# A four-layer graph network on one core: the gate computed first, edge terms gathered in layer 0, counts rounded by two instructions, waited values masked

## What is computed

```python
h = jnp.maximum(_layernorm(x), 0.0)
x = x + _L0_gnn_ref(h, src, dst, ...)       # relu((h + segment_sum(h[src], dst)) @ W1 + b1) @ W2 + b2
h = jnp.maximum(_layernorm(x), 0.0)
x = x + _L1_gnn_ref(h, edge_attr_64, ...)   # attention over the edges, 8 heads, softmax per target
h = jnp.maximum(_layernorm(x), 0.0)
x = x + _L2_gnn_ref(h, ...)                 # h @ w_self.T + mean of neighbours @ w_neigh.T
h = jnp.maximum(_layernorm(x), 0.0)
x = x + _L3_gnn_ref(h, src, dst, edge_weight, ...)   # segment_sum(edge_weight * h[src], dst) @ W + b
```

## Time and profile before

| | |
|---|---|
| three runs, without the profiler | 5042.48, 5067.97, 5065.54 us; median 5065.54 |
| the profiled execution | span 5145.3 us from its first to its last instruction; the page gives no other time of it, and it is 79.8 us above the median |
| PE, PEld, DVE, ACT, POOL busy | 75%, 53%, 74%, 30%, 53% of the span |
| mean granted clock of TensorE | 0.909 |
| DMA | 912 MB, 177 GB/s |

### The profile page before, as it was taken

One profiled execution on the slowest core, in us unless ns is written; L12 is line 12 of the kernel. 1 busy time (PEld: TensorE's weight loads), 2 busy tenths in 40 slices (PEclk: granted clock), 3 DMA queues, 4 the chain that ended last, 5 costly groups with the idle time before them and its releaser, 6 DMA issues. The chain is left out here.

```text
span 5145.3 us, 93266 instructions
## 1 busy us (share of the span) xinstructions
PE 3841.6 (75%) x26234; PEld 2720.9 (53%) x26235; DVE 3822.7 (74%) x6359; ACT 1550.3 (30%) x3023; POOL 2737.6 (53%) x2300
## 2 busy tenths in 40 slices
PE   4685555550199968888888888888886348889999
PEld 2443222220189835555555555555554248888888
DVE  3516999991299989999999999999996699970000
ACT  2372234560101130122333444445552430020000
POOL 3430199996732227777777777777776232210000
PEclk8799999995599989999999999999997569999999
DMA  9674423346155444454555666666665535568887
GB/s 168 175 234 111 97 100 126 159 175 198 66 193 209 163 140 106 120 146 142 157 165 169 184 184 188 193 196 197 205 204 159 186 113 200 200 213 300 298 297 254
DMA packets 594376, 912.02 MB, mean 177 GB/s; under 512 B 107452, under 2 KB 519442, under 8 KB 575022
## 3 DMA queue, kind: packets, MB, share of 16 engines
q1 hardware_dynamic: 413024, 521.23, 31.2%
q10 hardware_dynamic: 117359, 250.68, 13.4%
q0 software_dynamic: 63872, 138.75, 11.3%
HBM read 608.33 MB, written 311.94 MB: 179 GB/s over the span
## 5 line engine op out<-in xcount | busy, mean ns | idle before, releaser
L1964 POOL DMA_INDIRECT at_qg<-q_d,at_slot x1616 | 1601.2, 991 | 495.8 <-issue 492.2
L986 PE MATMUL bw_ps<-bw_mov,bw_sta 128*128 128x392 bf16 x7056 | 1590.0, 349 | 19.2 <-issue 7.2
L986 PEld LDWEIGHTS bw_ps<-bw_mov,bw_sta 128*128 128x128 bf16 x7056 | 640.4, 102 | 365.0 <-issue 95.6
L2007 PE MATMUL at_psk<-at_kp,at_hot 128*128 x4848 | 611.7, 234 | 286.8 <-DVE at_qg L2085 244.4
L1051 POOL DMA_INDIRECT tv_rows<-ed_d,tv_place x101 | 628.2, 6219 | 339.1 <-DMA edv_d<-tv_rows 211.0
L2007 PEld LDWEIGHTS at_psk<-at_kp,at_hot 128*128 128x128 bf16 x4848 | 439.1, 101 | 624.1 <-issue 418.1
L889 PE MATMUL ba_ps<-ba_mov,ba_sta 128*128 128x392 bf16 x1968 | 380.4, 338 | 352.6 <-DVE ba_sta L830 309.1
L874 DVE TENSOR_SCALAR ba_mov<-iota,key,scale 128x392 bf16<-128x392 f16 x1968 | 592.4, 365 | 2.8 <-PEq L853 2.8
L970 DVE TENSOR_TENSOR bw_sta<-bw_raw,kw 128x1024 bf16<-128x1024 bf16 x882 | 561.2, 689 | 0.0
L830 DVE TENSOR_TENSOR bw_mov<-bw_ps,lo 128x3136 bf16<-128x3136 f16 x294 | 523.4, 1780 | 7.6 <-PE bw_ps L986 5.4
L1566 PE MATMUL at_p3t<-tile,room 128*128 128x256 f32 (+1 forms) x2450 | 524.2, 376 | 4.6 <-ACT room L1150 4.6
(11 more groups left out here) (537 smaller groups left out, 4668.3 us busy)
## 6 DMA issues: line engine op xcount, KB each, us to landing
tile<-adw_d SPq DMA_DIRECT2D x23, 6272.0 KB, 18.7
adw_d<-xall ACTq DMA_DIRECT2D x65, 1568.0 KB
adj_d<-ba_stage ACTq DMA_DIRECT2D x50, 1568.0 KB, 5.1
l0raw<-adj_d SPq DMA_DIRECT2D x50, 1568.0 KB, 6.6
tile<-adj_d SPq DMA_DIRECT2D x50, 1568.0 KB, 6.5
adw_d<-bw_stage ACTq DMA_DIRECT2D x33, 1568.0 KB
at_rel<-rel_d SPq DMA_DIRECT2D x101, 512.0 KB
et_attr<-in_edge_attr SPq DMA_DIRECT2D x48, 1024.0 KB
```

Of the source, the lines that this page charges most:

```text
L986: ins = pe.matmul(self.ps[:, bass.DynSlice(place, WCOL)], self.sta[:, k, u // 2, :, u % 2], self.mov[:, u // 2, :, u % 2], start=False, st ...
L1964: pool.indirect_dma_start(out=qg[:, ring, b, :], out_offset=None, in_=q_d[:, :], in_offset=bass.IndirectOffsetOnAxis(ap=slot[:, ring, b:b ...
L2007: ins = pe.matmul(ps_k[:, at:at + KW], hot[:, par, sum(ROUNDS[:r]) + u, :], kp[:].rearrange("p j k n -> p (j k n)")[:, bass.DynSlice(place ...
```

## The change

Five things are changed.

- **The gate first.** `load_gate` is called ahead of `mask_rows`, with a semaphore of its own; POOL starts the counts' stage with the gate; SP waits for the store of the gate.
- **The gathers in layer 0.** `terms_by_visits` becomes a class with two buffers in place of four. POOL issues two gathers in each step of layer 0 behind its own three instructions (and its loop over the steps is written out), ACT stores them to `edv_d` at the head of its next step, in place of SP.
- **Rounding by two instructions**, in both layers with counts: one over 48 blocks, one over the last.
- **Masks.** The register values that PE and ACT wait for are masked with 2^14 - 1 first, in the counts and in the weights.
- The first weights' semaphore no longer covers the gate's inputs.

```diff
-        pe.wait_ge(self.s_clear, reg)
+        pe.wait_ge(self.s_clear, reg & TABLE)
...
-                act.wait_ge(self.s_vis, ends[k % half] + self.ring)
+                act.wait_ge(self.s_vis, (ends[k % half] & TABLE) + self.ring)
...
+class TermsByVisits:
+
+
+    def places(self):
+        wait(self.nc.gpsimd, self.c.V(self.nc.vector.tensor_copy(self.place[:], self.c.index[:, :, UK])))
+
+    def gather(self, g):
+        pool, k, lap = self.nc.gpsimd, g % self.ring, g // self.ring
         if lap:
-            pool.wait_ge(s_kept[k], 16 * lap)
-        pool.indirect_dma_start(out=rows[:, k, :], out_offset=None, in_=c.ed_d[:, :], in_offset=bass.IndirectOffsetOnAxis(ap=place[:, g:g + 1], axis=0)).then_inc(s_got[k], 16)
-        sp.wait_ge(s_got[k], 16 * lap + 16)
-        sp.dma_start(c.edv_d[g], rows[:, k, :]).then_inc(s_kept[k], 16)
-    for k in range(ring):
-        sp.wait_ge(s_kept[k], 16 * len(range(k, NG2, ring)))
+            pool.wait_ge(self.s_kept[k], 16 * lap)
+        pool.indirect_dma_start(out=self.rows[:, k, :], out_offset=None, in_=self.c.ed_d[:, :], in_offset=bass.IndirectOffsetOnAxis(ap=self.place[:, g:g + 1], axis=0)).then_inc(self.s_got[k], 16)
+
+    def keep(self, g, k, lap):
+        act = self.nc.scalar
+        act.wait_ge(self.s_got[k], 16 * lap + 16)
+        act.dma_start(self.c.edv_d[bass.DynSlice(g, 1), :, :].rearrange("a p n -> (a p) n"), self.rows[:, k, :]).then_inc(self.s_kept[k], 16)
+
+    def kept(self):
+        for k in range(self.ring):
+            self.nc.scalar.wait_ge(self.s_kept[k], 16 * len(range(k, NG2, self.ring)))
...
+        gate_sb = lambda n, shape: ctx.enter_context(nc.sbuf_tensor(n, shape, F32))
+        c.gate_loaded = load_gate(nc, c, a, gate_sb)
         mask_rows(nc, c)
         load_first_weights(nc, c, a)
-        terms_by_visits(nc, c, ctx)
-        Gate(nc, c, lambda n, shape: ctx.enter_context(nc.sbuf_tensor(n, shape, F32))).run()
+        Gate(nc, c, gate_sb).run()
...
-def load_gate(nc, c, a):
-
-    sp, L, t = nc.sync, c.L, c.gate_in
+def load_gate(nc, c, a, sb):
+
+    CH = 32
+    sp, L = nc.sync, Line(c.sem("gate_here"))
...
-        wait(pool, self.c.first_weights.loaded)
+        wait(pool, self.c.gate_loaded)
...
-        self.c.L.dma(sp.dma_start(self.c.gate_d, self.sums[:].rearrange("p j h -> p (j h)")))
+        self.c.gate_kept = Line(self.c.sem("gate_kept")).dma(sp.dma_start(self.c.gate_d, self.sums[:].rearrange("p j h -> p (j h)")))
+        wait(sp, self.c.gate_kept)
...
-        q.odd.inc(ve.tensor_scalar(cast[:, :, HALF:P], raw, ROUND, -ROUND, ALU.add, ALU.add))
+        ve.tensor_scalar(cast[:, 0:NB - 1, HALF:P], raw[:, 0:NB - 1, :], ROUND, -ROUND, ALU.add, ALU.add)
+        q.odd.inc(ve.tensor_scalar(cast[:, NB - 1, HALF:P], raw[:, NB - 1, :], ROUND, -ROUND, ALU.add, ALU.add))
...
-    def act(self):
+    def act(self, terms=None):
         def body(i, k, lap):
+            if terms and here(i - 1, NBV):
+                for t in range(2):
+                    at = 2 * (k - 1) + t
+                    terms.keep(2 * i - 2 + t, at % terms.ring, lap // (STEADY // RAW) * (2 * STEADY // terms.ring) + at // terms.ring)
             if here(i, NBV):
                 self.low_part(i, k)
             if here(i - 2, NB):
                 self.turned_sum(i - 2, k - 2)
             if here(i - 3, NB):
                 self.e.read_middle(self, i - 3, k - 3)
+        assert not terms or 2 * STEADY % terms.ring == 0
         in_steps(self.nc.scalar, body, NB + 3)
+        if terms:
+            for g in range(2 * NBV, NG2):
+                terms.keep(g, g % terms.ring, g // terms.ring)
+            terms.kept()
...
-    def pool(self, first):
+    def pool(self, first, terms=None):
         pool = self.nc.gpsimd
 
         def body(i, k, lap):
@@ -1476,8 +1499,18 @@
                 self.own_rows(i - self.e.own_lag, k - self.e.own_lag)
             if isinstance(i, int) and i == 1:
                 first()
+            if terms and here(i, NBV):
+                for g in range(2 * i, min(2 * i + 2, NG2)):
+                    terms.gather(g)
         self.q.high.wait(pool, NB // 7)
-        in_steps(pool, body, max(NBV, NB + self.e.own_lag))
+        steps = max(NBV, NB + self.e.own_lag)
+        if terms:
+            for i in range(steps):
+                body(i, i % STEADY, i // STEADY * (STEADY // RAW))
+            for g in range(2 * NBV, NG2):
+                terms.gather(g)
+        else:
+            in_steps(pool, body, steps)
...
+    terms = TermsByVisits(nc, c, lambda n, shape, dt=F32: sb("tv" + n, shape, dt))
     layer.sp()
+    terms.places()
```

32 lines of the change are left out of this document (13 added, 19 removed).

## The result

The changed kernel took 5253.52 us (median of 4 executions, 5247.90 to 5254.86), the kernel before 5066.76 (4 executions, 5042.48 to 5109.06). The ratio is 1.036, with a 95% interval of 1.033 to 1.039: 187 us slower, where 77 us less were forecast. The profiled execution of the changed kernel took 5253.72 us, its span is 5251.9.

A forecast was written before the change was run, and what follows sets the result against it. DVE was taken to bound most stages, with 190 us of POOL working alone after the counts. Terms -112 + 48 - 28 + 15 = -77 us, from the median 5065.54, gave 4989 us; range 4915 to 5095.

The forecast's parts named there:

- What bounds the kernel now: Whole kernel by stage: DVE busy nearly throughout the counts, layers and weights, then 190 us with POOL alone working.
- The 190 us: Between counts and layer 0, 1178 to 1368 us: POOL alone works, on late gathers and then 82.2 us of gate.
- The counts, -112: Counts: gathers leave, gate goes first; stage ends at 1256 instead of 1368 us, bounds -127 and -95.
- the upper bound: Counts: if gate and DVE take turns, DVE ends 82 us later and the stage ends at 1260.
- So I let 5 us of it show: Counts: masks add 0.26 to 0.74 us per eight visits on PE, busy 378.91 of 723 us; 5 us charged.
- The gathers in layer 0, +48: Layer 0: two gathers per step through two buffers make a step 8.6 instead of 7.64 us; bounds -26 and +158.
- The second rival: Layer 0: the ring binds hard, step 10.8 us, layer +158, sum +33, 5099 us; chance 0.12.
- the fifth: Layer 0: faster L1360 shuts the gathers out, step 10.4 us, sum +13, 5079 us; chance 0.04.
- The rounding, -28: Layer 2: L1360 falls from 3.41 to 1.75 us, step from 8.1 to 7.5; bounds -45 and 0.
- The masks in the weights, +15: Weights: a register instruction more per visit is just covered, as DVE sets the pace; +15 us, 0 to +60.

The follow-up runs named there:

- the run with two masks: Kernel before with masks, but PE waits on two masked registers per group of eight visits instead of eight: 5049 us, ten executions from 5010 to 5149.
- the run with the gate in the first stage: Kernel before with the masks and the gate moved to the first stage, where POOL is idle, gathers still in the counts: 5034 us.
- the third and fourth set: Two sets of runs in which every kernel took a quarter longer; the kernel before took 6457 and 6368 us.

## Why the prediction was wrong

The forecast was 4989 us, and the changed kernel took 264 more. By the stages above, 80 of them are the base, 56 the counts, 126 layer 0, 12 what lies between layer 0 and the weights, 18 the weights; layer 2 took 24 off, the rest 4. Layer 0 is the largest step that failed.

**What bounds the kernel now: right as a reading, wrong as a base.** The 190 us were there. But by the two groups of times, and by the run with two masks, which has the same scatter, they are probably a matter of how many gathers get in beside DVE, and differ by some 80 us between executions. The prediction noticed that its execution lay 79.8 us above the median and took the difference off the whole without asking which stage held it; most likely it was the stage whose end it then removed. In that case 80 us of the sum were counted twice, and the counts' term from the median is about -56 + 80 = +24 us. No trace of a faster execution of that kernel shows it.

**The counts, -112: failed.** The gate beside DVE cost 55 to 58 us, less than the 82 that the upper bound allowed for, since a third of the visits was still made. "So I let 5 us of it show" is the sentence that failed: the masks cost about 80 us there (82 by the run with the gate in the first stage; 0.32 us per eight visits, at 3.26 us a round instead of 2.94, give 76 for the visits not beside the gate). The price of one was right, 32 ns and 93 with what lies between, and it was held against the wrong cover: PE's array was busy for half of the time, but its queue was not free for the other half. Eight visits take it 8 x 0.25 us, and it issues nothing for about 1 us more between two groups, 3.0 us together, which is more than DVE's 2.94. That this 1 us is the loading of registers and the loop is likely and not shown. The term's bounds, -127 and -95, don't follow from their working either: 1239 and 1260 with the store's 2 us and the masks' 5 give -122 and -101.

**The gathers in layer 0, +48: failed, at +174 beyond its highest bound of 158.** The step came to 11.5 us, not 8.6. That the loop through the buffer binds was right in part: the third buffer gives back 58 of the 174 us. What was missing is what happens when it does: ACT's copy, late behind the landing of a gather, takes away the overlap of DVE's unpacking and PE's product, so that the step isn't lengthened by the lateness but by a whole unpacking. The steps of 13.8 us in the trace show this; no run took the wait off ACT. The second rival, a hard ring, was nearest (10.8 us); the fifth, DVE's faster form holding up the gathers, was part of the same outcome with some 60 us, and had been priced as an alternative to it.

**The rounding, -28: right in kind, low in size.** L1373 and L1374 take 1.75 and 0.19 us, 1.94 where 1.75 were taken. Layer 2 fell to 7.12 us a step, the value of a step held by PE alone, and gave 52 us, below the lower bound of -45. POOL was held as feared (4.41 us for a tile of 1.23 in layer 0, 2.53 in layer 2), but nothing waits for it there. By this the page VectorE: DVE Perf Modes of the Trainium skill, section "Mode 2×_2P — use both read ports for one tensor", was right for this shape.

**The masks in the weights, +15: right.** The stage took 2037 us in the kernel before, 2041 with the masks alone, and 2038 to 2070 over the kernels with all eight masks, the third and fourth set left out. The changed kernel took 2070 and, a second time, 2045 there, so its 33 us are not all the masks'; what sets the rest was not found.

**The gate's time beside DVE.** The Trainium skill, SBUF — State Buffer, section "Who interferes with whom", gives an exclusive lock. The traces agree in that DVE is held: its longest one-hot instruction takes 4.43 us with the masks alone, 0.38 in the median. The gate wins most of its turns: with the masks alone 88 instructions on DVE in 85 us, where 261 fit in the run with two masks (770 to 855 us).

## What to carry to other kernels

If the profiled execution is slower than the median, find the stage that holds the difference before pricing anything in that stage; compare the scatter of the times with what could cause it. An instruction on an engine's queue is paid from the queue's free time, not from the array's: count a round of the queue and set it against the round of the engine that sets the pace. Work put on an in-order engine ahead of a copy that releases another engine's next unit can cost more than its own lateness: the overlap that the copy made possible. Moving it to the end of the step was not enough here, since the next copy stood behind the same wait.

## What was not expected of the hardware

- POOL's gathers and POOL's arithmetic meet the same busy DVE very differently: gathers were held for 93, 211, 224, 245 and 279 us beside a stream of DVE instructions without pauses, while the gate's 52 instructions ran in 85 us and took two thirds of DVE's turns. With all eight masks, where DVE pauses now and again for 1 to 2 us, none of 101 gathers took over 1.62 us. But beside a DVE without pauses 83 gathers in a row also took at most 1.26 us, so what shuts a gather out is not known.
- The slower PE queue went together with executions that agree: 5091 to 5101 us with the masks alone, 5018 to 5152 without.
- The granted clock fell to 0.52, close to the lower of its two levels (1.2 of 2.4 GHz), in the stretch of the gate, while PE made 72 visits in 85 us, and was 0.83 in layer 0 with its idle times, 0.98 before. The 49 products that start at 1607.41, behind PE's idle time, take 7.59 us; those at 1595.04, close behind others, 6.12.
- In two sets of runs a visit took 1.40 us while gathers were in flight, and the stage of the weights 3302 to 3322 us instead of 2040; in a set nine minutes later, on the same chip as the second of them, both were as usual. What sets it was not found.
